# Attention scores and row maxima of a two-layer transformer kernel in two 64-row halves of TensorE

## The reference

```python
def reference(x, ...):                     # x is [4, 256, 512]
    xn = _layernorm(x)
    x = x + _L0_attn_ref(xn, Wq, Wk, Wv, Wo) + _L0_ffn_ref(xn, W1, b1, W2, b2)
    xn = _layernorm(x)
    x = x + _L1_attn_ref(xn, w_qkv, b_qkv, w_dense, b_dense) + _L1_ffn_ref(xn, w12, b12, w3, b3)
    return x

# both attentions: 32 query heads, 8 key/value heads, head size 16, 256 positions
attn = einsum('bhqd,bhkd->bhqk', q, k) * scale
attn = softmax(attn, axis=-1)              # layer 1: causal mask before it, rotary q and k
out = einsum('bhqk,bhkd->bhqd', attn, v)
# L0_ffn: gelu(x @ W1 + b1) @ W2 + b2, inner size 2048
# L1_ffn: (silu(x1) * x2) @ w3.T + b3 with x1, x2 = split(x @ w12.T + b12), inner size 512
```

## Time and profile before

| | us |
|---|---|
| median of 3 runs | 597.12 |
| lowest and highest | 596.23 to 598.24 |
| profiled execution, own time | 596.43 |
| its span | 594.7 |
| PE busy | 563.2 (95%) |
| DVE busy | 456.5 (77%) |
| ACT busy | 348.0 (59%) |
| POOL busy | 232.6 (39%) |

### The profile page before, as it was taken

The page is one execution under the profiler, slowest core; times in us unless marked ns, Lnnn a source line. Parts: engine busy times, 40 slices in busy tenths (PEclk is TensorE's granted clock), DMA queues, the critical chain, the costliest instruction groups (busy, mean ns, idle before and its releaser), DMA issues.

```text
span 594.7 us, 10503 instructions
## 1 busy us (share of the span) xinstructions
PE 563.2 (95%) x3216; PEld 435.0 (73%) x3216; DVE 456.5 (77%) x1232; ACT 348.0 (59%) x598; POOL 232.6 (39%) x345
## 2 busy tenths in 40 slices
PE   3979999999999999999999999899899999998997
PEld 3967777777777878777787787667677778766754
DVE  6487987765666687577899678898998989789673
ACT  3667756664564676376677276357645564565451
POOL 6231334713304521313223115264745485364242
PEclk9999999999999999999999999999999999999999
DMA  6993452453223244315433323336443443434101
GB/s 200 130 317 103 120 142 69 113 157 107 79 82 108 80 124 136 90 40 174 126 128 99 113 78 101 90 107 143 134 117 89 104 130 109 125 108 133 29 6 68
DMA packets 30535, 67.02 MB, mean 113 GB/s; under 512 B 4880, under 2 KB 18192, under 8 KB 28560
## 3 DMA queue, kind: packets, MB, share of 16 engines
q1 hardware_dynamic: 21840, 38.04, 24.5%
q0 software_dynamic: 8640, 28.32, 15.9%
HBM read 50.87 MB, written 13.63 MB: 108 GB/s over the span
## 4 chain that ended last, share of the span: by engine, by line
PE 79%; DVE 8%; issue 5%; DMA 3%; POOL 2%; ACT 2%; DVEq 0%; POOLq 0%; ACTq 0%
PE banks L766 53%; PE banks L826 8%; PE banks L874 8%; PE banks L852 7%; DMA q_sb<-max_t 2%; DVE banks L1156 2%; PE banks L786 1%; PE banks L855 1%; POOL probs L708 1%; DVE neg_max L1156 1%; DVE o_tok L1177 1%; DVE x_res L1200 1%; PE banks L835 1%; DVE bn L1054 1%; DVE hid L1221 1%
## 5 line engine op out<-in xcount | busy, mean ns | idle before, releaser
L988 ACT ACTIVATE probs<-banks 128x512 f32<-128x512 f32 (+1 forms) x256 | 138.0, 545 | 187.5 <-PE banks L852 149.2
L766 PE MATMUL banks<-xnT,w_up 128*128 128x512 f32 x576 | 153.8, 400 | 0.2
L1161 DVE TENSOR_REDUCE neg_max<-banks 128x2 f32<-128x512 f32 x128 | 87.4, 688 | 79.3 <-PE banks L826 77.9
L766 PE MATMUL banks<-w_down,hid 128*128 128x512 f32 x480 | 127.4, 399 | 0.0
L766 PEld LDWEIGHTS banks<-xnT,w_up 128*128 128x128 f32 x576 | 102.1, 190 | 30.6 <-issue 12.9
L826 PEld LDWEIGHTS banks<-k_sb,q_sb 96*128 96x128 f32 x512 | 92.5, 191 | 23.6 <-issue 5.5
L1156 DVE CUSTOM_DVE_ANT_0 banks<-banks,mask_qk 128x128 f32<-128x128 f32 (+1 forms) x256 | 86.3, 375 | 25.5 <-PE banks L826 24.9
L826 PE MATMUL banks<-k_sb,q_sb 96*128 96x256 f32 (+1 forms) x512 | 100.0, 277 | 5.4 <-issue 3.2
L766 PEld LDWEIGHTS banks<-w_down,hid 128*128 128x128 f32 x480 | 85.2, 188 | 25.7 <-DVE max_t L1169 5.9
L708 POOL TENSOR_SCALAR_AFFINE_SELECT probs<-probs 128x256 f32<-128x256 f32 x128 | 59.5, 465 | 75.9 <-ACT probs L988 69.3
L852 PE MATMUL banks<-q_sb,k_sb 97*128 97x512 f32 x192 | 78.8, 410 | 8.4 <-DMA q_sb<-max_t 7.0
(11 more groups left out here) (79 smaller groups left out, 655.3 us busy)
## 6 DMA issues: line engine op xcount, KB each, us to landing
q_sb<-q_parts SPq DMA_DIRECT2D x60, 256.0 KB, 4.8
raw<-in_up POOLq DMA_DIRECT2D x48, 256.0 KB, 3.4
raw<-in_down POOLq DMA_DIRECT2D x40, 256.0 KB, 3.1
q_parts<-stage SPq DMA_DIRECT2D x30, 256.0 KB, 2.5
raw<-in_attn POOLq DMA_DIRECT2D x20, 256.0 KB, 3.6
k_parts<-stage SPq DMA_DIRECT2D x14, 256.0 KB, 2.5
k_sb<-k_parts SPq DMA_DIRECT2D x14, 256.0 KB, 4.1
out<-x_res SPq DMA_DIRECT2D x8, 256.0 KB, 2.1
```

What stands on the lines that cost most here:

```text
L766: mm = nc.tensor.matmul(out_ap, lhs(a), rhs(b_), start=first and j == 0, stop=stop and j == 2, **kw)
L988: nc.scalar.activation(probs[:, i, 0:w], banks[:, ST_BANKS[k % 2], 0:w], ACT.Exp, scale=SCALES[n // B]).then_inc(exp_done, 1)
L1161: nc.vector.tensor_reduce(neg_max[:, s, 2 * g:2 * g + 2, t], banks[:, bank_of[x], :].rearrange("p (r t) -> p r t", r=2)[:, :, 0:w], AX.X, ...
```

## The change

The contraction of `m` and `st` shrinks to 48 rows (three products of high and low parts, no zeros) and 49 with the maximum's row. Even and odd key/value heads of a unit lie at partitions 0 to 48 and 64 to 112 of `q_sb` and `k_sb`; a step issues its matmuls in turn for the two halves `a` = 0 and 1 of PE, each half into a bank of its own. A step does the work of two old ones: four steps of `st` in the even slots, into the banks 0 and 1 together, four of `m` in slots 0, 2, 4 and 6, each taking two work banks at once. The number of matmuls and their columns are the same as before. `COST` of `st` and of `m` is now 340 for a step. `mt` and `mrow` move from slot 5 to slot 3. The queries have a ring of four and are loaded a unit earlier (`load_q(u+3)` in slot 6), with four DMAs of 32 and 16 rows in place of two; the keys have two whole buffers, and a load is two DMAs. The maxima's row takes two DMAs. `pv(u-1, 1)` moves to slot 0 and `pv(u, 0)` to slot 4 in L0, to slots 2 and 6 in L1. The copies that set rows of `q_sb` to zero (`fill`) are gone; loads of later inputs (`load_x`, `load_bias`) move from the start into units 0 and 1. The gate and hidden steps of L1's feed-forward come one slot with an `st` later. The scratch tensors in DRAM have other layouts, and the order of the heads in the weights follows.

```diff
+HALF = 64
+ROWS = 48
+MROW = 48
-MT_SLOT = 5
+MT_SLOT = 3
+Q_RING = 4
-COST = {"up": 681, "down": 681, "wo": 693, "qkv": 363, "xn": 440, "v": 220, "st": 233, "m": 235, "mt": 110, "pv": 995}
+COST = {"up": 681, "down": 681, "wo": 693, "qkv": 363, "xn": 440, "v": 220, "st": 340, "m": 340, "mt": 110, "pv": 995}
...
+        j = i // 2
+        if i % 2 == 0:
+            slots[i].append(("st", u, j))
+        if i == 0 and u + 1 < UNITS:
+            slots[i].append(("m", u + 1, 3))
+        if i in (2, 4, 6) and u + 2 < UNITS:
+            slots[i].append(("m", u + 2, j - 1))
         if i == MT_SLOT and u + 1 < UNITS:
             slots[i] += [("mt", u + 1), ("mrow", u + 1)]
...
+        slots[0 if u < LU else 2].append(("pv", u - 1, 1))
...
+    slots[4 if u < LU else 6].append(("pv", u, 0))
...
-        q_sb = sb("q_sb", [P, RING, UH, T], F32R)
-        k_sb = sb("k_sb", [P, NKV, T], F32R)
+        q_sb = sb("q_sb", [P, Q_RING, UH // 2, T], F32R)
+        k_sb = sb("k_sb", [P, 2, NKV // 2, T], F32R)
...
                     for r in range(2):
-                        mm = nc.tensor.matmul(banks[:, k, r * T:r * T + w],
-                                              q_sb[0:ROWS, u % RING, 2 * g + r, t * P:t * P + P], k_sb[0:ROWS, 4 * f + g, 0:w],
-                                              start=r == 0, stop=r == 1, skip_group_check=True)
+                        for a in range(2):
+                            rows = slice(HALF * a, HALF * a + ROWS)
+                            mm = nc.tensor.matmul(banks[:, ks[a], r * T:r * T + w],
+                                                  q_sb[rows, u % Q_RING, 2 * c + r, t * P:t * P + P], k_sb[rows, n % 2, 2 * f + c, 0:w],
+                                                  start=r == 0, stop=r == 1, skip_group_check=True)
                     mm.then_inc(wk_filled, 1)
...
+                    if st_index(u, j):
+                        pe.wait_ge(exp_done, 2 * st_index(u, j))
...
+                    for a in range(2):
+                        rows = slice(HALF * a, HALF * a + MROW + 1)
+                        mm = nc.tensor.matmul(banks[:, ST_BANKS[a], 0:2 * (T - q0)].rearrange("p (r t) -> p r t", r=2),
+                                              k_sb[rows, n % 2, 2 * f + c, t * P:t * P + P],
+                                              q_sb[rows, u % Q_RING, 2 * c:2 * c + 2, q0:], start=True, stop=True)
                     mm.then_inc(st_filled, 1)
```

More of the change, by code:

```diff
@@ L121, in with_followers @@
             for d, y in followers(x):
+                if d == STEP:
+                    d = [k for k in range(1, 4) if g + k >= len(slots) or any(z[0] == "st" for z in slots[g + k])][0]
                 if d == 0:
@@ L678, in _ @@
             pool.wait_ge(made, ALL_MADE)
-            done = [(made, ALL_MADE)]
+            for k, row in enumerate((32, HALF + 32)):
+                nc.gpsimd.memset(k_sb[row:row + 32, 1, :, :].bitcast(F32), 1.0).then_inc(made, 1)
+                pool.wait_ge(made, ALL_MADE + 1 + k)
+            done = [(made, MORE_ONES)]
             def in_order():
@@ L758, in work @@
             def work(x):
-                if before[x]:
-                    wait_fill_read(pe, before[x])
+                for y in before[x]:
+                    wait_fill_read(pe, y)
                 return bank_of[x]
@@ L987, in _ @@
                     w = 2 * P if n >= B and t == 1 else 512
-                    nc.scalar.activation(probs[:, i, 0:w], banks[:, ST_BANKS[k % 2], 0:w], ACT.Exp,
-                                         scale=SCALES[n // B]).then_inc(exp_done, 1)
+                    for a in range(2):
+                        nc.scalar.activation(probs[:, 2 * j + a, 0:w], banks[:, ST_BANKS[a], 0:w], ACT.Exp,
+                                             scale=SCALES[n // B]).then_inc(exp_done, 1)
                 if x[0] == "ctx":
```

354 lines of the change are left out of this document (180 added, 174 removed).

## The result

The changed kernel takes 606.01 us, the median of six runs (601.71 to 610.01), against 597.16 us of the kernel before beside it; the ratio is 1.0148 [1.0102, 1.0194]. The profiled execution took 604.32 us, with a span of 602.5. So the kernel is 1.5% slower, where 576 us (546 to 592) had been predicted.

A forecast was written before the change was run, and what follows sets the result against it. PE was taken to bound the kernel, with DVE close in L1. From the profiled 596.4 us: -17.4 (PE's queue) -3 (start) -2.5 (maxima's waits) +2 (new waits) = 575.5, median 576 us; range 546 to 592.

The forecast's parts named there:

- The streams: PE's st and m: both halves run at once, a group's streams take 0.48 us against 0.94, gross saving 0.46.
- term of 17.4 us: PE's queue in both layers: halves' saving less partition changes, 10.2 us in L0 and 7.2 in L1.
- cheap changes: Rival: partition changes on PE cost little, as at mt; 546 to 565 us, chance 0.25.
- weights one after another: Rival: weight loads of the two halves queue, some 0.18 us more a group; 599 us, chance 0.08.
- no overlap: Rival: the halves stream one after another, so only partition changes are paid; 632 us, chance 0.08.
- L0: Stage from 60 to 360 us: PE saves 0.64 us a unit, 10.2 us over 16 units.
- L1: Stage from 360 to 580 us: PE saves 0.45 us a unit, 7.2 us over 16 units.
- The maxima's waits: Remaining 2.7 us of st waits for the maxima's DMA go, mrow having five slots instead of three; 2.5 us saved.
- The start: First st comes at 39.5 us, 2.2 earlier, plus 0.8 of low clock regained; 3 us saved, bounds -2 and +5.
- Waits: New waits in L1 for work banks and for both exponentials of a pair; 2 us added (0 to 10).
- DVE and banks take L1: Rival: in L1 PE waits about 1 us more a unit for DVE or exponentials; 592 us, chance 0.07.
- price of a change of partition: On PE, entering or leaving full-width matmuls costs 0.20 us; said to carry 20 of the 59 us between cases.

The follow-up runs named there:

- e17: Kernel before with a light load: POOL's tensor operations cut to 16 or 32 columns, L1's maxima over 64 keys; 586.88 us, ratio 0.9822.
- e12: Changed kernel with POOL's tensor operations cut to 16 or 32 columns, L1's maxima over 64 keys, load_q(2) two steps earlier; 572.92 us, ratio 0.9596.
- e14: e13 with score and maxima matmuls at full height (112 and 114 rows) in the same order; 606.62 us, ratio 1.0168.
- e13: e8 with the edits of e9 and e11 together, nothing left out; 589.29 us, ratio 0.9872.
- e5: Changed kernel, same order and DVE work, with every m and st matmul at full height (112 and 114 rows); 618.20 us, ratio 1.0370.
- e7: Kernel before with four waits of PE put into L0, each on ten POOL memsets; 622.56 us, ratio 1.0437.
- e1: Changed kernel with mt and mrow back in slot 5, nothing else; 605.53 us, ratio 1.0153.
- e9: e8 with the maxima of both layers in their old slots and mt in slot 5; 594.38 us, ratio 0.9977.
- e8: Changed kernel with load_q(2) ahead of the first maxima's row on SP's queue and one sequence's statistics a unit later; 597.70 us, ratio 1.0028.
- e11: e8 with all low parts of the weights subtracted on DVE, none on POOL; 594.26 us, ratio 0.9964.
- e2: Kernel before, full height, with st and m two by two in the even slots; 602.27 us, ratio 1.0067.

## Why the prediction was wrong

**The streams: right.** Overlap of the halves (3 to 4 ns between the starts of a pair), `m` pairs 0.12 apart, and 0.09 to 0.10 us late with 0.10 to 0.11 us of uncovered weights at each change of partition, 0.20 us, were read as forecast. The term of 17.4 us can be checked with PE's busy time less 0.41 us for each us of low clock: e17 against e12 560.5 - 2.9 - (543.4 - 2.8) = 17.0 us; e14 against e13 18.7; e5 against after (570.9 - 11.1) - (554.7 - 12.3) = 17.4; before against after (563.2 - 1.5) - (554.7 - 12.3) = 19.3. These are estimates, since the 0.41 is from one run; all lie within 2 us of the term. With 0.52 outside the waits they are 17 to 21. The rivals "cheap changes", "weights one after another" and "no overlap" all fall with it.

**L0: right in size, hidden by stalls.** 10.2 us were forecast; with the load light in both kernels (e17, e12) L0 is 311.5 - 299.7 = 11.8 us shorter. As the change stands it is 1.4, since 5.2 us of new idle time and 8.6 us at the low clock (3.5 us by e7's 0.41) came in: 10.2 - 5.2 - 3.5 = 1.5.

**L1: the work was saved, the time hardly.** 7.2 us were forecast. Between e17 and e12 PE's busy time in L1's window falls by 3.2 us with 2.8 us more work in it, some 6 us. But L1 itself gained about 4 us there, 2.0 between e14 and e13, and nothing as the change stands: 210.9 us against 203.1. PE's waits for `neg_max` in L1 alone are 11.4 us, for `max_t` 6.4, where the prediction had named growth beyond 2 us as the sign that L1's term is wrong.

**The maxima's waits, -2.5: right.** They are gone from the waits of after and come back with `mt` in slot 5 (e1, e9).

**The start, -3: wrong.** The first `st` no longer waited, but it came at 41.54 us (41.73 before), not at 39.5: on its way PE waited 0.38 us for ACT, 1.11 for the first queries and 0.46 for `neg_max`. Then the second `m` behind it waited 3.51 us for `q_parts`, and ran at low clock behind it. I had looked at what stood ahead of the maxima's row on SP's queue and not at what then stood behind it, `load_q(2)`. Start and end together, which the slot of `mt` leaves alone, are 80.4 us against 79.0 before; with that load moved (e8) they are 74.7, 4.3 less than before.

**"Waits", +2 us (0 to 10): the step that failed.** PE's time without work grew by 16.3 us over the span (47.8 against 31.5), although about 7 us of old waits are gone. The step priced banks and exponentials one at a time, by the time that an operation of DVE takes alone. It missed three things. First, DVE's queue: at 86% in L1 the mean load was even below the forecast 88 to 90% (189.2 us of 220), but the order of what DVE did ahead of `neg_max` and `max_t` was not followed; moving the maxima by a step put `max_t` behind weights and rotary products. Second, DVE's operations are up to nine times longer beside POOL's (1.52 for 0.16 us), and PE, by now faster and with half as many and twice as large requests for banks, met them at once, in L0 too, where I had put no wait at all.

Third, **the price of a stall is not its length.** The forecast had one term for the clock, 0.8 us to be won back at the start, and none for a clock that falls behind new stalls. Some 26 us more at the low level cost about 11 us by e7's 0.41. The account of the whole then closes: 16.3 us of idle time, 10.8 of clock, -19.3 of streams are the +7.8 us by which the span grew (the last term comes from the same busy times, so the closing proves nothing by itself; the streams rest on the 17.0 to 18.7 of the other pairs). Against the forecast, which had the profiled execution 20.9 us faster, 28.8 us are missing: some 19 are idle time and some 12 clock, and the streams gave 2 back.

**The rival "DVE and banks take L1"** (592, chance 0.07) named the mechanism and was mis-sized: 1 us a unit, no clock, and L1 alone. The forecast took the price of a change of partition for its weakest point, and that price was right; its closing "20 of the 59 us" does not come out of its own sum, in which the streams bring 128 x 0.46 = 59 and the changes take 38.

What stays open is which part of the remaining waits of e13 an order could take away. It is also open whether the 4 us that L1 grew by when the start was changed (e8) are more than scatter; the same L1 took 211.6 in e11. The 21 us that the order without halves costs were not divided up: pairs (e2) are some 5 of them, the place of the maxima some more (e9), and the rest was not taken apart. That the low clock costs the same per us in every kernel was not shown, nor why the same order has less of it at full height (e14) than with halves (e13).

## What to carry to other kernels

When a change makes the bounding engine quicker and its steps coarser, follow the queue of the next engine step by step at two or three places, with the durations that it has beside its neighbour, before putting a wait at 2 us; a mean load of 86% says nothing about who stands ahead of whom. Seven of eight stalls of 2.3 to 3.5 us on TensorE were followed here by work at half the clock, so count such a stall at more than its length. And test such a change with the other engines made light in both kernels: that separates its own worth (14 us here) from what the order takes back.
